# Causal attention: four heads' queries in one tile, scores from 32 rows each, issued for two heads at a time

## The chip, the cores and the metric

The kernel runs on one core of a Trainium2 chip. The time is the device time of one execution in microseconds. The kernel is one program with sixteen stages one after another; the change touches one of them. The engines are called PE (TensorE), DVE (VectorE), ACT (ScalarE), POOL (GpSimd) and SP (SyncE).

## The reference, cut to what matters

The whole computation is a chain of graph and feed-forward layers. The stage at issue is the causal self-attention of the fourth layer: 4 query heads of 32 features over 2 key and value heads, rotary positions, on 16 sequences ("graphs") of 512 tokens with 128 features, all in fp32. The reference text gives its sizes and its rotary tables:

```python
NH, NKV = (4, 2)
HD = C // NH            # C = 128
def _rope_tables(t_len):
    inv_freq = 1.0 / 10000.0 ** (np.arange(0, HD, 2, dtype=np.float32) / HD)
...
def _rotate_half(x):
    h = x.shape[-1] // 2
    return jnp.concatenate([-x[..., h:], x[..., :h]], axis=-1)
```

In words: x is normalised by its mean square, projected to q, k and v; q and k are rotated (q*cos + rotate_half(q)*sin); scores are q k^T / sqrt(32) with only earlier tokens allowed; softmax; times v; output projection; plus x.

## The kernel before, in words

`mha_stage` (L306) with `rope=True` is called once, as stage "mha3". It has one group of four heads. A head has 32 features, so the 128 partitions hold the four heads, 32 each. A graph has 16 items (`items`), one for each of 4 query tiles of 128 tokens and each of 4 heads: item n has head n % 4 and query tile `ORDER[n // 4]`, with ORDER (2, 0, 1, 3). The causal limit makes the items 384, 128, 256 and 512 keys wide, four of each in this order. `all_graphs` runs graph 0, then pairs of graphs in a loop, then graph 15.

Each engine has its own instruction list, and they meet only by semaphores. For item n:

- PE, `scores` (L487): one fp32 matmul from `qT[s][j]` and `kT[s]` into one of two PSUM banks, `score[n % 2]` (an fp32 matmul is two MATMUL records with a weight load each). It waits for `score_taken`, that DVE has taken item n-2 from that bank. Item 0 waits also for `rot_ready`, the rotated k of this graph.
- DVE, `graph` (L800): the "take": score plus mask and the row minimum, into `prob[n % 4]`; after even n a copy of the transposed item n-3 (odd) out of PSUM (L697). A take waits until the transposes of item n-4 are done.
- ACT (L635): the exponential of item n, and after odd n the copy of the transposed item n-3 (even, L606).
- PE, `transposes` (L504): three items behind (`LAG`), one 128x128 transpose for each 128 keys.

`qT[s][j]` is a 128x512 tile for each head j, with the head's 32 rows filled and the other 96 zero. The matmul contracts over all 128 rows against `kT`, which holds all four heads; the zeros take out the other three. The zeros are written once, by eight DVE memsets (L682). With an item n of graph b, PE also issues at fixed places (`at`) a step of the other chains: after item 3 `values` of graph b-1 (L518, 32 matmuls on four column tiles), at 4 `back_rows` (L527), at 6 `turn_ctx` (L533), at 7 `project_out` (L539), at 8 `project_v` (L473), at 9 `rows_in` of graph b+1 (L449), at 10 and 12 two projections each (`early`, L468) of graph b+1. Within one n, `scores(b, s, n)` stands first, then `values`, `transposes(n - 3)`, then the others.

The rotation of graph b+1: PE projects q, q half turned, k, k half turned into the two `misc` banks. DVE multiplies them by the tables (L714, in `rotate`), two at n = 11 and two at n = 13, into `part`. POOL adds the two q products (L409), as four additions of 32 rows, one per head, and then the two k products (L413) into `kT`. At n = 15 DVE has the last step of the statistics, a 128x8 copy (L789), before the take.

## Time and profile before

| | |
|---|---|
| time, median of 3 runs | 5262.46 us (5259.3 to 5265.08) |
| the profiled execution: time / span | 5262.09 us / 5260.3 us |
| PE / DVE / ACT / POOL busy in the span | 75% / 55% / 39% / 32% |
| scores of the stage, L496 (512 records) | 192.6 us busy |
| transposes of the stage, L504 (640 records) | 118.0 us busy |
| takes of the stage, L800 (256) | 125.2 us busy |
| q additions, L409 (64) | 80.9 us busy |
| stage "mha3" in the span | 4088 to 4655 us |

A line of the timeline is one or several instructions of one line of code in a row: start in us from the span's start, length, engine, line, operation, what is written and read, number, and in brackets the idle time of that engine before it and what ended it. Matmul records end with a modelled tail, so the next one can start before the end of one. Windows give the busy time of each engine and the granted clock of PE as a share of 2.4 GHz.

### The profile page before, as it was taken

How to read it: one execution, taken by the hardware profiler on the slowest of the kernel's cores; microseconds unless marked ns; L12 is line 12 of the kernel's file. 1: busy time of each engine (PE TensorE's matmuls, PEld its weight loads, DVE VectorE, ACT ScalarE, POOL GpSimd, SP SyncE). 2: the span in 40 equal slices, each digit the busy share in tenths (PEclk: the TensorE clock that was granted, in tenths of full speed). 3: DMA queues.
4: the chain of work that ended last, by engine and by line, in shares of the span. 5: the costliest groups of instructions: out<-in, count | busy, mean ns of one | idle time of the engine just before them, and what ended most of it. 6: DMA issues, size and time to landing. Idle time of an engine off the chain costs nothing. (4 is left out here: it accounts for less than half of the span.)

```text
span 5260.3 us, 85948 instructions
## 1 busy us (share of the span) xinstructions
PE 3924.9 (75%) x25676; PEld 2535.6 (48%) x25676; DVE 2902.3 (55%) x10746; ACT 2062.9 (39%) x5230; POOL 1658.4 (32%) x1801
## 2 busy tenths in 40 slices
PE   3999978888888539999886776169665677751995
PEld 1333337777777313333364565147554344431663
DVE  5666644444444766666477876322377555543344
ACT  1666643333333005666532266234355344431321
POOL 3445410000000024544362122745522321236444
PEclk9999985555555659999998988589888899965997
DMA  4333349000000023333100021134431000001444
GB/s 131 107 103 111 101 165 382 0 0 0 0 0 0 0 73 104 109 111 98 36 0 1 0 97 41 47 114 145 148 104 41 1 0 0 0 22 51 131 128 157
DMA packets 237304, 376.22 MB, mean 72 GB/s; under 512 B 24832, under 2 KB 157056, under 8 KB 228672
## 3 DMA queue, kind: packets, MB, share of 16 engines
q1 hardware_dynamic: 218688, 336.03, 20.4%
q0 software_dynamic: 18432, 38.05, 2.1%
q8 instruction: 77, 1.26, 0.1%
q14 instruction: 107, 0.88, 0.1%
HBM read 210.37 MB, written 163.61 MB: 71 GB/s over the span
## 5 line engine op out<-in xcount | busy, mean ns | idle before, releaser
L1343 DVE CUSTOM_DVE_ANT_0 mha_seen<-mha_score,mha_mask 128x512 f32<-128x512 f32 x1024 | 686.6, 688 | 454.4 <-PE mha_score L1114 451.5
L1246 ACT ACTIVATE mha_prob<-mha_turned 128x512 f32<-128x512 f32 x1024 | 608.8, 601 | 489.7 <-PE mha_turned L1125 459.3
L1114 PE MATMUL mha_score<-mha_k_rows,mha_q_rows 96*128 96x512 bf16 x1024 | 396.9, 390 | 56.1 <-DVE mha_low L1343 27.8
L3025 POOL DMA_INDIRECT expert_rows<-expert_y,expert_target x320 | 306.4, 957 | 371.6 <-DVE expert_y L3160 155.7
L1124 PE MATMUL mha_turned<-mha_maskT,core_ident_bf 128*128 128x512 bf16 x1024 | 392.8, 384 | 4.6 <-ACT mha_prob L1246 3.5
L1125 PE MATMUL mha_turned<-mha_q_rows,mha_k_rows 99*128 99x512 bf16 x1024 | 390.7, 382 | 0.0
L1498 PE MATMUL lstm_gates<-lstm_h_part,lstm_w_part 128*128 128x16 f16 x4608 | 270.6, 179 | 124.5 <-DVE lstm_h_part L1660 124.4
L1498 PEld LDWEIGHTS lstm_gates<-lstm_h_part,lstm_w_part 128*128 128x128 f16 x4608 | 230.3, 109 | 212.1 <-DVE lstm_h_part L1660 165.1
L1491 PE MATMUL lstm_gates<-lstm_xg,core_ident 128*128 128x48 f32 x1024 | 328.2, 421 | 0.7 <-ACT lstm_xg L1566 0.7
L1448 POOL TENSOR_TENSOR core_mid<-lstm_hist,lstm_per_unit 128x256 f32 x32 | 23.5, 733 | 942.8 <-DVE lstm_hist L1661 942.8
L2698 POOL DMA_INDIRECT routed_rows<-route_rows,core_slot x256 | 253.5, 990 | 151.6 <-issue 78.7
L1652 DVE SCALAR_TENSOR_TENSOR lstm_prod<-lstm_act 128x32 f32<-128x32 f32 x512 | 98.4, 192 | 364.5 <-ACT lstm_act L1572 364.5
L1493 PE MATMUL lstm_out_gates<-lstm_xg,core_ident 128*128 128x16 f32 x1024 | 293.9, 368 | 0.0
L3063 PEld LDWEIGHTS expert_out_ps<-expert_w,expert_hid 128*128 128x128 f32 (+1 forms) x2240 | 262.5, 192 | 38.6 <-issue 36.0
L1493 PEld LDWEIGHTS lstm_out_gates<-lstm_xg,core_ident 128*128 128x128 f32 x1024 | 279.9, 333 | 0.0
L1135 PE MATMUL mha_o<-mha_prob,mha_v 128*32 128x512 f32 x2048 | 272.8, 605 | 1.4 <-ACT mha_prob L1246 1.4
L3063 PE MATMUL expert_out_ps<-expert_w,expert_hid 128*128 128x128 f32 (+1 forms) x2240 | 262.7, 275 | 0.0
L635 ACT ACTIVATE mha_prob<-mha_prob,mha_bias 128x384 f32<-128x384 f32 (+3 forms) x256 | 143.8, 562 | 302.5 <-DVE mha_bias L800 302.1
L800 DVE CUSTOM_DVE_ANT_0 mha_prob<-mha_score,mha_mask 128x384 f32<-128x384 f32 (+3 forms) x256 | 125.2, 489 | 247.2 <-PE mha_tpose L504 126.0
L1491 PEld LDWEIGHTS lstm_gates<-lstm_xg,core_ident 128*128 128x128 f32 x1024 | 257.7, 312 | 1.3 <-issue 1.3
L1572 ACT ACTIVATE lstm_act<-lstm_gates 128x48 f32<-128x48 f32 x512 | 106.5, 208 | 328.4 <-PE lstm_gates L1498 328.4
L1124 PEld LDWEIGHTS mha_turned<-mha_maskT,core_ident_bf 128*128 128x128 bf16 x1024 | 99.5, 97 | 265.5 <-ACT mha_prob L1246 182.6
(477 smaller groups left out, 9130.4 us busy)
## 6 DMA issues: line engine op xcount, KB each, us to landing
routed_rows<-lstm_blank SPq DMA_DIRECT2D x66, 1040.0 KB, 24.9
core_params<-adj SPq DMA_DIRECT2D x32, 1024.0 KB, 5.9
gat_adj_raw<-adj SPq DMA_DIRECT2D x32, 1024.0 KB, 5.5
mha_q_rows<-split_rows SPq DMA_DIRECT2D x64, 384.0 KB, 4.6
mha_k_rows<-split_rows SPq DMA_DIRECT2D x64, 384.0 KB, 5.5
expert_x<-routed_rows SPq DMA_DIRECT2D x80, 260.0 KB
expert_w<-weights SPq DMA_DIRECT2D x80, 256.0 KB
combine_pair<-expert_rows SPq DMA_DIRECT2D x32, 512.0 KB, 4.9
```

Of the source, the lines that this page charges most:

```text
L1114: pe.matmul(score[n % 2][:, :], rows[0][s][0:ROWS, h, t * P:(t + 1) * P], rows[1][s][0:ROWS, h, :], start=True, stop=True).then_inc(S["sco ...
L1124: pe.matmul(turned[n % 2][:, :], core.ident_bf[:, :], maskT[s][:, u, :], start=True, stop=False)
L1125: pe.matmul(turned[n % 2][:, :], rows[1][s][0:ROWS + 3, h, u * P:(u + 1) * P], rows[0][s][0:ROWS + 3, h, :], start=False, stop=True).then_ ...
L1135: last = pe.matmul(o_ps[g][32 * j:32 * j + 32, :], v32[s][:, u, 4 * g + j, :], prob[:, (4 * quad + j) % RING, :], start=(u == 0), stop=(u ...
L1246: act.activation(prob[:, n % RING, :], turned[n % 2][:, :], ACT.Exp, scale=-1.0).then_inc(S["prob_ready"], 1)
L1343: dve.tensor_tensor_reduce(seen[n % 2][:, :], score[n % 2][:, :], mask[1 - s][:, t, :], 1.0, 3e38, ALU.add, ALU.min, low[g][:, t, j:j + 1] ...
L1491: pe.matmul(gates[t % 2][:, 0:3 * B], core.ident[:, :], xg[s][:, t, 1:4, :].rearrange("p g b -> p (g b)"), start=True, stop=False)
L1493: pe.matmul(out_gates[t % 2][:, 0:B], core.ident[:, :], xg[s][:, t, 0, :], start=True, stop=False)
L1498: return pe.matmul(out, w[:, g * P:(g + 1) * P], h_part[:, part, :], start=False, stop=(part == 1 and n in (0, 3)))
L2698: pool.indirect_dma_start(out=rows_dram[:, :], out_offset=bass.IndirectOffsetOnAxis(ap=core.slot[:, i, n:n + 1], axis=0), in_=out_rows[s][ ...
L3025: pool.indirect_dma_start(out=core.y_rows[NUMBER][:, :], out_offset=bass.IndirectOffsetOnAxis(ap=target[q][:, t:t + 1], axis=0), in_=y_buf ...
L3063: last = pe.matmul(out_ps[q % 2][:, t * D:(t + 1) * D], hid[q % 2][0:wid, h, t * P:(t + 1) * P], w_buf[q][0:wid, at2 + h * D:at2 + (h + 1) ...
```

## The change

One tile `qT[s]` holds the queries of all four heads. A score matmul reads the 32 rows of its head from `qT[s]` and from `kT[s]`, so it uses 32 rows of the array, at row 32j. POOL makes `qT[s]` with one addition of 128 rows instead of four of 32. The memsets and their semaphore go. PE issues the scores of items n and n+1 together, at each even n, so that an odd item's matmul, and its wait for `score_taken`, stands ahead of the steps that came between the two. The two items of a pair have different rows and different PSUM banks.

```diff
-        qT = [[m.sb(f"qT{g}{j}", [P, N]) for j in range(4)] for g in range(2)]
+        qT = [m.sb(f"qT{g}", [P, N]) for g in range(2)]
...
                     pool.wait_ge(S["qk_ready"], 4 * b + 2 + 1)
-                    if first:
-                        pool.wait_ge(S["zeros_set"], 8)
-                    for j in range(4):
-                        rows = slice(32 * j, 32 * j + 32)
-                        pool.tensor_tensor(qT[s][j][rows, :], part[rows, 0, :], part[rows, 1, :], ALU.add)\
-                            .then_inc(S["rot_ready"], 1)
-                    pool.wait_ge(S["rot_ready"], 5 * b + 4 + 5)
+                    pool.tensor_tensor(qT[s][:, :], part[:, 0, :], part[:, 1, :], ALU.add).then_inc(S["rot_ready"], 1)
+                    pool.wait_ge(S["rot_ready"], 2 * b + 1 + 2)
                     pool.wait_ge(S["qk_ready"], 4 * b + 4 + 1)
...
                 if n == 0 and rope:
-                    pe.wait_ge(S["rot_ready"], 5 * b + 5 + 5)
+                    pe.wait_ge(S["rot_ready"], 2 * b + 2 + 2)
...
                 pe.wait_ge(S["score_taken"], items * b + n + 1)
                 width = keys(t) * P
                 pair = s if rope else g
-                pe.matmul(score[n % 2][:, 0:width], qT[pair][j][:, t * P:(t + 1) * P], kT[pair][:, 0:width], start=True, stop=True)\
+                head = slice(32 * j, 32 * j + 32)
+                pe.matmul(score[n % 2][:, 0:width], qT[pair][head, t * P:(t + 1) * P], kT[pair][head, 0:width], start=True, stop=True)\
                     .then_inc(S["score_done"], 1)
...
             def graph(b, s, first=False, last=False):
                 for n in range(items):
-                    scores(b, s, n)
+                    if n % 2 == 0:
+                        scores(b, s, n)
+                        scores(b, s, n + 1)
                     if n == at["values"] and not first:
...
-            for q in qT:
-                for j in range(4):
-                    dve.memset(q[j][:, :], 0.0).then_inc(S["zeros_set"], 1)
...
                 if half_ == 0:
-                    dve.wait_ge(S["rot_ready"], 5 * b + 5)
+                    dve.wait_ge(S["rot_ready"], 2 * b + 2)
```

The rest of the diff changes a branch for `rope=False`, which this program doesn't call.

## Rows read from the trace of the kernel before

**Rows 1.** Windows of two neighbouring graphs: busy us (instructions), clock
```profile
4239.70:4273.00 33.30, 24.02 (x141) 14.78 (x141) 18.48 (x60) 13.94 (x42) 7.34 (x7) 1.00 0.00 0
4273.00:4308.00 35.00, 25.60 (x141) 15.76 (x141) 18.67 (x60) 14.02 (x42) 7.34 (x7) 0.95 0.00 0
```

**Rows 2.** PE timeline of the first: start, length, engine, line, operands, idle before
```profile
4239.72 0.91 PE L496 MATMUL mha_score<-mha_kT,mha_qT 128*128 128x384 f32 x2 [1.88 <-POOL mha_kT L413]
4240.46 0.60 PE L504 MATMUL mha_tpose<-core_ident,mha_prob 128*128 128x128 f32 x4
...
4244.43 2.36 PE L518 MATMUL mha_o<-mha_probT,mha_v 128*32 128x512 f32 x32 [0.45 <-DVE mha_probT L697]
...
4254.02 1.16 PE L539 MATMUL mha_misc<-core_params 128*128 128x128 f32 x8 [1.63 <-ACT core_params L628]
...
4258.45 0.63 PE L449 MATMUL mha_misc<-core_ident,core_params 128*128 128x128 f32 x4 [1.29 <-DVE mha_v L721]
...
4261.42 1.99 PE L468 MATMUL mha_misc<-core_params 128*128 128x512 f32 x4 [1.79 <-DVE core_params L705]
...
4265.53 1.98 PE L468 MATMUL mha_misc<-core_params 128*128 128x512 f32 x4 [0.40 <-DVE core_params L714]
4267.35 1.02 PE L496 MATMUL mha_score<-mha_kT,mha_qT 128*128 128x512 f32 x2
4268.22 0.38 PE L504 MATMUL mha_tpose<-core_ident,mha_prob 128*128 128x128 f32 x2
...
4272.98 1.46 PE L496 MATMUL mha_score<-mha_kT,mha_qT 128*128 128x384 f32 x2 [1.87 <-POOL mha_kT L413]
```

**Rows 3.** DVE timeline of the same graph
```profile
4243.59 0.69 DVE L697 COPY mha_probT<-mha_tpose 128x512 f32<-128x512 f32 x1
...
4250.16 0.29 DVE L800 CUSTOM_DVE_ANT_0 mha_prob<-mha_score,mha_mask 128x128 f32<-128x128 f32 x1 [1.67 <-PE mha_score L496]
...
4265.39 0.68 DVE L714 TENSOR_TENSOR core_params<-mha_misc,mha_nsin 128x512 f32<-128x512 f32 x1
...
4268.60 0.69 DVE L800 CUSTOM_DVE_ANT_0 mha_prob<-mha_score,mha_mask 128x512 f32<-128x512 f32 x1 [1.19 <-PE mha_tpose L504]
...
4269.50 1.26 DVE L714 TENSOR_TENSOR core_params<-mha_misc,core_params 128x512 f32<-128x512 f32 x2
...
4271.62 1.26 DVE L789 COPY core_x_stat<-mha_two 128x8 f32 x1
4272.79 0.68 DVE L800 CUSTOM_DVE_ANT_0 mha_prob<-mha_score,mha_mask 128x512 f32<-128x512 f32 x1
```

**Rows 4.** POOL timeline at the end of the same graph
```profile
4266.16 5.27 POOL L409 TENSOR_TENSOR mha_qT<-core_params 32x512 f32<-32x512 f32 x4 [25.57 <-DVE core_params L714]
4271.59 1.26 POOL L413 TENSOR_TENSOR mha_kT<-core_params 128x512 f32<-128x512 f32 x1 [0.16 <-POOL mha_qT L409]
```

**Rows 5.** DVE timeline in the last graph, with POOL idle
```profile
4639.26 0.16 DVE L789 COPY core_x_stat<-mha_two 128x8 f32<-128x8 f32 x1
```

**Rows 6.** Timeline of all engines at the start of the stage
```profile
4091.83 4.27 DVE L682 MEMSET mha_qT<- 128x512 f32 x8 [0.50 <-issue]
...
4096.36 1.09 PE L449 MATMUL mha_misc<-core_ident,core_params 128*128 128x128 f32 x4 [58.19 <-POOL core_params L401]
...
4104.18 0.69 DVE L714 TENSOR_TENSOR core_params<-mha_misc,core_params 128x512 f32<-128x512 f32 x1 [0.16 <-PE mha_misc L468]
...
4109.63 1.01 PE L496 MATMUL mha_score<-mha_kT,mha_qT 128*128 128x384 f32 x1 [5.49 <-POOL mha_kT L413]
```

**Rows 7.** PE timeline in the first attention stage, around column tiles
```profile
331.58 0.38 PE L1125 MATMUL mha_turned<-mha_q_rows,mha_k_rows 99*128 99x512 bf16 x1
331.80 0.38 PE L1114 MATMUL mha_score<-mha_k_rows,mha_q_rows 96*128 96x512 bf16 x1
332.10 1.06 PE L1135 MATMUL mha_o<-mha_prob,mha_v 128*32 128x512 f32 x8
333.10 0.39 PE L1124 MATMUL mha_turned<-mha_maskT,core_ident_bf 128*128 128x512 bf16 x1
```

More of the change, by code:

```diff
@@ L431, in _ @@
             if rope:
-                pool.sem_inc(S["rot_ready"], 5)
+                pool.sem_inc(S["rot_ready"], 2)
             all_graphs(pool, graph)
@@ L598, in _ @@
                 act.wait_ge(S["const_set"], 1)
-                act.wait_ge(S["zeros_set"], 8)
             def copy_probT(b, n):
@@ L615, in take_qk @@
                 else:
-                    for j in range(4):
-                        rows = slice(32 * j, 32 * j + 32)
-                        ins = act.activation(qT[g][j][rows, :], bank[rows, :], ACT.Identity, bias=neg_bq[rows, g:g + 1],
-                                             scale=-scale)
+                    ins = act.activation(qT[g][:, :], bank[:, :], ACT.Identity, bias=neg_bq[:, g:g + 1], scale=-scale)
                 ins.then_inc(S["qk_ready"], 1)
@@ L679, in _ @@
             dve.wait_ge(core.params_in[k], 16)
-            for q in qT:
-                for j in range(4):
-                    dve.memset(q[j][:, :], 0.0).then_inc(S["zeros_set"], 1)
             dve.memset(v32[:, :, :, :], 0.0).then_inc(S["v32_set"], 1)
```

## The prediction, made before the changed kernel was run

> **What bounds the kernel now.** The change touches only the rope attention stage (`mha_stage`, tag mha3), some 550 us of the span from 4090 us on. So I read that stage alone, once the page had shown its slices. First the stretches of two neighbouring graphs [rows 1]: one takes 33.3 us at a granted clock of 1.00, the next 35.0 us at 0.95. PE is the busiest engine (24.0 of 33.3 us), but it is idle for 9.3 us, DVE for 15, POOL for 26. No engine is full; the stage is a chain that passes between them. Of the 15 intervals from one graph's S0 to the next, 6 are of the 35.0 kind, so a fall of the clock costs 1.7 us and comes about in every second graph.
>
> Then PE's timeline of the undisturbed graph [rows 2]. Its waits show where the chain lies: S0 (score matmul of item 0) waits 1.88 us for POOL's kT; the output projection (L539), the turned rows (L449) and the first rotary projections (L468) wait 1.63, 1.29 and 1.79 us for copies by ACT and DVE. I cut the graph at four of these: S0 to values (4239.72 to 4244.43) 4.71 us; values to output projection (4254.02) 9.59; to the turned rows (4258.45) 4.43; to the next S0 (4272.98) 14.53. Sum 33.26.
>
> Last the other two engines at the graph's end. The second rotation on DVE starts at 4269.50 after a wait of 1.19 us for item 13 [rows 3]. POOL's four q additions take 5.27 us from 4266.16, so kT begins only at 4271.59 [rows 4], though the rotation it needs ended at 4270.7. A 128x8 copy on DVE (L789) that starts inside kT's run takes 1.26 us [rows 3]; another, with POOL idle, takes 0.16 [rows 5]. So I read that copy as held until POOL's addition ends.
>
> **Part 1: four q additions become one.** A 32x512 addition takes 5.27/4 = 1.3 us, the 128x512 one for kT 1.26 [rows 4]: cost follows the row length, not the rows. Three of four vanish, 4.0 us of POOL per graph. On the path this is worth less: kT must still wait for the second rotation. Before, kT began 0.9 us after it; after, 0.15 (the step from nsin's end to the first q addition). Gain by this part alone 0.75 us per graph.
>
> **Part 2: no zeros, no memsets.** Eight memsets take 4.27 us of DVE at the stage's start, to 4096.1 [rows 6]. PE's first matmul starts at 4096.36 and waited for POOL's xn, and DVE's next step needs that matmul. POOL's work hides the memsets: gain nothing. The stage's start gains by part 1: the second rotation ends at 4104.8, kT then runs 4104.95 to 4106.2 and S0 starts at 4106.3 instead of 4109.63 [rows 6]: 3.3 us, once.
>
> **Part 3: 32 rows instead of 128.** A score matmul streams the same columns with fewer rows; alone it gains nothing that a row shows. What can gain is that two of them occupy different rows of the array. No row tile is in the trace. The nearest row is the column tiles: eight 512-column fp32 passes on four tiles take 332.10 to 333.10 us, 1.00 us [rows 7], where the two 512-wide fp32 passes of one item on the full array take 0.87, from item 13 at 4267.35 to the transposes at 4268.22 [rows 2]; so four tiles ran nearly together. I take full overlap of the two heads, with none as the other bound. One 512-wide item costs 0.87 us, so 128, 256 and 384 cost 0.22, 0.43, 0.65; a graph's 16 items cost 8.6 us of PE, and paired 4.3.
>
> Against it stands the change of array shape. Into the column tiles the step was 0.30 us [rows 7] where neighbouring full-array steps are 0.22: 0.08 lost. The eight passes, with the way out, took 1.00 us for two passes' 0.87: about 0.1 lost. The tile form appears and leaves eight times per graph, since transposes on the full array stand between pairs. I take 0.1 us for each, bounds 0 and 0.3 (a full exposed weight load and drain). The Trainium skill, TensorEngine Tiling (Array Packing), section Key Properties, says that changing the tiling mode drains the engine. The trace agrees, with 0.08 to 0.1 us.
>
> **Part 4: S(n+1) is issued with S(n).** This moves each odd score ahead of the transposes, projections and values that stood between. Its wait (DVE has taken item n-1) now stands ahead of all of these on PE. I walk the graph with it.
>
> *Rows to next S0.* S10 and S11 follow the turned rows together (+0.1 for the shape). xT's chain on DVE is as before: projections 0 and 1 start at 2.97+0.1 = 3.07 and take 1.99 with tail [rows 2]. Before, item 11 stood behind them and DVE had to take it before the rotation; now it is done. The nsin product begins at 3.07+1.99+0.15 = 5.2 and ends at 5.8 (before 66.0-58.45 = 7.5). S12 and S13 start at 5.2, take 0.87 together, T9 follows, projections 2 and 3 start at 6.6 (before 7.08). DVE takes item 12 at 5.2+1.25 = 6.45 (1.25 is S13 to its take, 4267.35 to 4268.60 [rows 2, 3]). From take 12, which follows nsin at 4266.0, to the rotation (4269.50) DVE had 3.51 us, 1.19 of it the wait for S13, which is gone: 2.32 us. Rotation from 8.77 to 9.95 (before 70.7-58.45 = 12.25). kT 10.1 to 11.35, S0 at 11.5. Before 14.53: gain 3.0.
>
> *S0 to values.* Here the new wait bites: S1 needs item 15 taken. Before, from the rotation's end (4270.7) to take 15 (4272.79) were 2.1 us, with the copy's 1.2. After: take 14 and a copy, 0.95, to 10.9; the 128x8 copy held until 11.4 by kT; take 15 to 12.05. So S1 starts at 12.15, 0.65 behind S0. T13 waits behind it: 12.9 to 13.35 (four transposes, 0.60 with their tail [rows 2]). DVE: copy 13 from 13.6 (0.6), take 1 (0.5) to 14.7. S3 waits for that: 14.8. T15 behind it at 15.55, done 16.2 with its latency, copy 15 (0.6), values at 16.95, which is 5.45 after S0, against 4.71: loss 0.75. (A 512-wide copy is 0.69 in its row and 0.6 from its start to the next one's, a 512-wide take 0.68; the 384-wide take is estimated from it at 0.5 [rows 3].)
>
> *Values to output projection.* S4 enters the shape: +0.1. The take of item 5, 0.29 and its 0.08 [rows 3], stood between the turned outputs and the normalisation, because S5 came behind them; now it lies ahead: -0.4; item 7 no longer starts behind the turned context: about -0.1. 9.15 for 9.59.
>
> *Output projection to rows.* DVE takes items 8 and 9 and v; only the small wait for item 9 goes: 4.2 for 4.43.
>
> **The sum.** 11.5+5.45+9.15+4.2 = 30.3 us for 33.3: 3.0 per graph. Fourteen full intervals give 42; the first gives about the same 3.0 (its first items have no copies before them); the stage's start 3.3; the last graph's loss at its head and gain behind cancel. 48 us. The profiled execution has 5262.09 us (its span 5260.3), 0.4 us from the median of the runs shown, 5262.46. 5262-48 = 5214.
>
> **Rivals.**
> - *The row tiles don't overlap; the change doesn't do what it says.* For: no row shows row tiles. Against: rows 7. Price: S12/S13 +0.87 ahead of the projections, of which DVE's own work covers a part (+0.55), and 0.15 elsewhere: +0.7 per graph, 11 in all: 5225. The forecast hangs little on overlap, since the gain comes from order.
> - *Changing the shape costs 0.3 us, not 0.1.* For: fp32 weights of 128 columns are larger than the 32 columns of rows 7. Six of sixteen changes lie on my walk: +1.2 per graph, 19 in all: 5233.
> - *Evacuation by DVE decides.* Both banks now fill together and empty one after the other; S(n+1) holds the transposes at more places than the head. For: the head shows it at 0.75 us. Against: at six of eight pairs both banks are free by my walk, and DVE is busy 18.5 of 33.3 us. Price, if three more pairs lose as much: +2.25 per graph, 36 in all: 5250. The Trainium skill, TensorEngine Tiling (Array Packing), section PSUM Bottleneck, states such a rule: tiling speeds up the matmuls, and the copy out of PSUM may then be the bound.
> - *The clock falls more often (slower).* PE will be busy about 20 of 30.3 us, 66% for 72% now, and with a lull of 2 us around S0 that is split by single short matmuls. Place: the stage's granted clock, between the two levels 2.4 and 1.2 GHz. A fall costs 1.7 us [rows 1], 6 are there now. It decides from (48+10)/1.7 = 34 falls, over two per graph; at four per graph 16x4x1.7-10 = 99 us: 5313. Against: the longest idle stretches of PE shrink from 1.88 us rather than grow, and the clock stays up between falls now with the same kind of gaps.
>
> **How the numbers follow.** Forecast 0.52 (own range 5196 to 5222), no overlap 0.14, costly shape 0.12, evacuation 0.12, clock 0.10. The low end is the forecast with no falls of the clock left (10 us less) and a change of shape that costs nothing (six on the path, 0.1 us each, 14 graphs, 8 us less): 5196. The high end takes in the costly shape with one fall per graph (9 falls more, 15 us): 5248. What is left out is the clock case and half of the evacuation case, under 2 in 10. About 0.2%, 10.5 us, is what a measurement of this kernel can tell from no change. Below 5251.9: the first three and most of the fourth, 0.84. Within: the rest of evacuation and a mild clock case, 0.08. Slower: 0.08.
>
> **What would show it.** Graph to graph 30.3 us on S0 or kT. POOL: one q addition of 1.26 us, kT within 0.2 us after the second rotation, PE's wait for kT still there, near 1 us. Score passes of two heads starting within 0.05 us of each other, but S1 some 0.6 us behind S0 and S3 behind S2. S0 to values longer, 5.4 us. The second rotation some 10 us after the turned rows. Stage's start to S0 3.3 us shorter. It is wrong if the pair's second matmul regularly waits for DVE, if the clock falls in each graph, or if the rotation still waits for item 13.

## The result, and the profile of the changed kernel

The changed kernel is slower: 5310.28 us (median; 5303.46 to 5317.51) against 5263.77 us of the kernel before on the same chip, a ratio of 1.009 (95% interval 1.0074 to 1.0106), 46.5 us more. The forecast was 48 us less.

First the page of the kernel after: its span, the busy time of the engines and the granted clock in 40 slices. Slices 32 to 35 lie wholly in the changed stage, and the clock is 0.7 in each; in the kernel before these slices have 0.8, 0.9, 0.9 and 0.9.

```profile
span 5315.8 us, 85891 instructions
PE 4000.6 (75%) x25676; PEld 2535.3 (48%) x25676; DVE 2891.7 (54%) x10738; ACT 2065.2 (39%) x5230; POOL 1600.2 (30%) x1753
PEclk8999975555555659999998896599797777765997
```

Next the table of windows. Columns: start and end, length; busy time and count of PE, PEld, DVE, ACT and POOL; granted clock; DMA share and GB/s. The kernel before, from the stage's first S0 to its last score matmul:

```profile
4109.60:4638.70 529.10, 389.66 (x2163) 239.30 (x2164) 285.62 (x919) 219.24 (x662) 109.76 (x90) 0.96 0.00 0
```

The kernel after: the same stretch, then two neighbouring graphs, then the first two rotary projections of the earlier of the two.

```profile
4106.50:4681.60 575.10, 467.05 (x2162) 244.89 (x2162) 277.97 (x918) 221.59 (x664) 52.89 (x45) 0.77 0.00 0
4287.60:4320.60 33.00, 25.54 (x140) 13.78 (x140) 17.75 (x60) 13.95 (x42) 3.45 (x4) 0.90 0.00 0
4320.60:4358.60 38.00, 31.25 (x140) 16.28 (x140) 17.25 (x58) 13.40 (x42) 3.60 (x4) 0.73 0.00 0
4309.70:4313.20 3.50, 3.48 (x4) 1.39 (x5) 1.39 (x5) 0.60 (x2) 0.00 (x0) 0.50 0.00 0
```

The stretch grew by 46.0 us, the size of the medians' difference, and it began 3.1 us earlier. (The two profiled runs, 5317.51 and 5262.09 us, differ by 12 us more than these account for. That lies in the stage behind: from the last score matmul to the last transfer into `routed_rows` it took 229 us for 215, and among all the kernels run here, none of which touches it, 203 to 230.) POOL's work halved, DVE's fell a little, PE's rose from 390 to 467 us with the same count of matmuls. The clock says why: 0.96 before, 0.77 after. With 0.5 for the low level, that is 8% of the stretch at 1.2 GHz before and 46% after. All 14 full intervals from S0 to S0 have the low clock in them: twelve last 36.8 to 38.8 us and two 33.1, mean 37.1. Before, eight of the 14 had none and took 33.3 us [rows 1].

By line, PE's matmuls of the stage, kernel after (line, engine, operation, tiles, count | busy us, mean ns | idle before):

```profile
L500 PE MATMUL mha_tpose<-core_ident,mha_prob 128*128 128x128 f32 x640 | 134.6, 326 | 0.9 <-ACT mha_probT L603 0.9
L463 PE MATMUL mha_misc<-core_params 128*128 128x512 f32 x128 | 99.2, 922 | 24.6 <-DVE core_params L696 24.6
```

and in the kernel before:

```profile
L504 PE MATMUL mha_tpose<-core_ident,mha_prob 128*128 128x128 f32 x640 | 118.0, 285 | 2.2 <-ACT mha_probT L606 2.1
L468 PE MATMUL mha_misc<-core_params 128*128 128x512 f32 x128 | 68.8, 664 | 33.8 <-DVE core_params L705 27.5 <-DVE core_params L714 6.3
```

Neither the transposes nor the projections were edited, yet one takes 326 ns for 285 and the other 922 for 664. Work that the change didn't touch became slower with the clock.

PE's timeline of the graph that starts at 4287.57, kernel after, answers to [rows 2]:

```profile
4287.57 1.46 PE L492 MATMUL mha_score<-mha_kT,mha_qT 32*128 32x384 f32 x4 [0.96 <-POOL mha_kT L408]
4288.96 1.14 PE L500 MATMUL mha_tpose<-core_ident,mha_prob 128*128 128x128 f32 x8
4290.02 1.75 PE L492 MATMUL mha_score<-mha_kT,mha_qT 32*128 32x384 f32 x4
...
4293.24 2.36 PE L514 MATMUL mha_o<-mha_probT,mha_v 128*32 128x512 f32 x32 [0.88 <-DVE mha_probT L688]
...
4302.24 1.16 PE L535 MATMUL mha_misc<-core_params 128*128 128x128 f32 x8 [1.68 <-ACT core_params L622]
...
4306.56 0.63 PE L444 MATMUL mha_misc<-core_ident,core_params 128*128 128x128 f32 x4 [1.27 <-DVE mha_v L712]
...
4309.72 3.78 PE L463 MATMUL mha_misc<-core_params 128*128 128x512 f32 x4 [1.64 <-DVE core_params L696]
...
4320.65 0.58 PE L492 MATMUL mha_score<-mha_kT,mha_qT 32*128 32x384 f32 x1 [0.96 <-POOL mha_kT L408]
```

Cut where the prediction cut, the graph has 5.67 us from S0 to values, 9.00 to the output projection, 4.32 to the turned rows: 18.99, where the walk had 18.8. Then the first two rotary projections (four records) take 3.78 us at a granted clock of 0.50, for 1.99 before [rows 2], and the last part takes 14.09 us instead of 11.5. In most graphs the low clock stays on into the next: there the same values matmuls take 3.85 us, not 2.36. The longest waits there (1.68, 1.27, 1.64 us) are about as long as those of [rows 2] (1.63, 1.29, 1.79), behind which the clock stayed up. Nor was PE less busy. Two windows show the first 20.93 us from S0, first in the undisturbed graph of the kernel before, then in this graph, up to its fall:

```profile
4239.72:4260.65 20.93, 14.70 (x110) 10.29 (x110) 9.99 (x36) 10.23 (x32) 0.86 (x1) 1.00 0.00 0
4287.57:4308.50 20.93, 15.59 (x112) 9.56 (x112) 9.58 (x34) 9.71 (x31) 0.87 (x1) 0.99 0.00 0
```

PE is busy for 70% of the first and 74% of the second, and only behind the second the clock falls. The falls are long, too. One of the kernel before, then the one above and the next:

```profile
4273.30:4276.80 3.50, 3.50 (x11) 2.09 (x10) 1.45 (x6) 1.99 (x5) 0.55 (x1) 0.53 0.00 0
4308.50:4315.30 6.80, 5.58 (x10) 2.12 (x10) 3.28 (x9) 1.57 (x5) 1.00 (x1) 0.53 0.00 0
4321.80:4332.00 10.20, 9.32 (x41) 4.63 (x44) 3.43 (x10) 3.88 (x12) 0.00 (x0) 0.50 0.00 0
```

Read in windows of 0.5 us (not shown), the 14 full intervals hold 26 such falls, 7 to 14 us each and 235 us in all; those of the kernel before hold 6, five of them of 3.4 us and one of 6.8, 24 us in all.

POOL in the same graph, answering to [rows 4]:

```profile
4314.30 1.26 POOL L405 TENSOR_TENSOR mha_qT<-core_params 128x512 f32<-128x512 f32 x1 [25.87 <-DVE core_params L705]
4319.25 1.27 POOL L408 TENSOR_TENSOR mha_kT<-core_params 128x512 f32<-128x512 f32 x1 [3.69 <-DVE core_params L705]
```

One q addition of 1.26 us for four of 5.27, and kT waits for the rotation and not for POOL. So POOL's part of the mechanism worked as told, and the clock took back more than the change gave.

### The profile page after: what moved, and what is told of

It is laid out like the page before. It is cut to its first block and busy times, and to the rows that moved or that the text cites. A ratio compares the mean times of both kernels' runs of the same rounds, so it can differ in the third digit from the quotient of the medians.

```text
span 5315.8 us, 85891 instructions
## 1 busy us (share of the span) xinstructions
PE 4000.6 (75%) x25676; PEld 2535.3 (48%) x25676; DVE 2891.7 (54%) x10738; ACT 2065.2 (39%) x5230; POOL 1600.2 (30%) x1753
## 3 DMA queue, kind: packets, MB, share of 16 engines
q8 instruction: 77, 1.26, 0.1%
```

## The experiments

The question: why does the clock fall in every graph, when PE's longest idle stretches didn't grow? Three theories. *Few rows*: a matmul from 32 rows of the array does not hold the clock as one from 128 does. *Shape*: changing between 32-row and full form, 16 times per graph, leaves holes (packing alone changes it 32 times). *Order*: issuing in pairs makes the lull around S0 worse. The stage column below is the stretch from first S0 to last score matmul in the profiled run, with its clock; the difference is that of the medians on the same chip. The kernel before took 5224 to 5280 us, depending on the chip, so only these differences can be set side by side.

### The change taken apart, and with the array kept at work

**Packing alone, old order** (against the kernel after):

```diff
                 for n in range(items):
-                    if n % 2 == 0:
-                        scores(b, s, n)
-                        scores(b, s, n + 1)
+                    scores(b, s, n)
```

> The changed kernel with the old order: packed queries, one POOL addition, scores from 32 rows, but each score matmul issued alone at its own n. Theory A (the clock falls because 32-row matmuls work a quarter of the array): falls in every graph as in the changed kernel, 35.5 to 37 us per graph, 5290 to 5320 us. Theory B (the clock falls because the pair order makes lulls on PE): clock as before, 0.75 us per graph less for POOL and about as much more for sixteen changes of the array's shape, 5255 to 5270 us. Theory C (not the clock, but changes of shape and the new wait): the sixteen changes alone, about 5270 us.

**Order alone** (against the kernel before: queries with zeros, all 128 rows, four q additions):

```diff
                 for n in range(items):
-                    scores(b, s, n)
+                    if n % 2 == 0:
+                        scores(b, s, n)
+                        scores(b, s, n + 1)
```

> The kernel before with the pair order alone: four zero-padded query tiles, four POOL additions, all 128 rows. Theory A: the clock stays up as before; by my walk the second rotation ends 2.3 us sooner but kT waits for POOL's four additions, S0 comes 1.7 us sooner, the head loses 0.75, the rest gains 0.6: 1.6 us per graph less, about 5238 us. Theory B: falls in every graph, 5290 us or more. Theory C: the new wait costs here too, 5265 to 5300 us.

**The kernel after with fillers**: 28 matmuls per graph whose result nobody reads, on 128 rows and in bf16, put where PE waits (4 ahead of S0, 3 of the values, 4 of the turned outputs, 6 of the output projection, 5 of the turned rows, 6 of the projections).

```diff
+            pe.wait_ge(S["adj_free"], 1)
+
+            def fill(count):
+                for _ in range(count):
+                    pe.matmul(o_ps[1][:, :], core.ident_bf[:, :], mask[0][:, 0, :], start=True, stop=True)
...
+                    if n == 0:
+                        fill(4)
...
                     if n == at["values"] and not first:
+                        fill(3)
                         values(b - 1, groups - 1)
```

> The changed kernel with 28 filler matmuls per graph (bf16, 512 columns, full array, into an unused PSUM bank), placed in PE's waits ahead of S0, values, the turned outputs, the output projection, the turned rows and the first projections. Theories A and B: the granted clock goes back to nearly 1.00 and the graph takes the 30.3 us of my walk, or up to 31.5 where a filler overlaps a wait's end: 5215 to 5240 us. Theory C: no gain, 5310 us or more.

**The kernel before with fillers**: 31 per graph at the same six places (7, 1, 5, 6, 5, 7).

> Control: the kernel before with 31 such fillers per graph in its waits. It has 6 to 9 short falls of the clock in the stage. If fillers hold the clock up they go: 10 us less, about 5253 us; if fillers cost time by themselves it is 5265 us or more.

| kernel | median us | before, same chip | ratio (95%) | difference | stage us, clock |
|---|---|---|---|---|---|
| packing alone | 5476.25 | 5279.73 | 1.038 (1.0363 to 1.0398) | +196.5 | 722.9, 0.67 |
| order alone | 5233.75 | 5279.73 | 0.9917 (0.990 to 0.9933) | -46.0 | 484.1, 0.99 |
| after, filled | 5226.95 | 5279.73 | 0.990 (0.9883 to 0.9916) | -52.8 | 479.0, 0.98 |
| before, filled | 5265.74 | 5279.73 | 0.9976 (0.9966 to 0.9985) | -14.0 | 514.9, 1.00 |

The order is innocent: it saves 46.0 us. Of these, 31 are its 14 graphs at 2.2 us each, and some 8 come from the clock, as two of its graphs have a fall where six had one. The packing does the harm, and far more than I had expected of few rows: 5476.25 us where I had 5290 to 5320. The windows of order alone, one graph and the whole stretch:

```profile
4265.60:4296.60 31.00, 23.79 (x140) 15.04 (x140) 18.72 (x60) 14.04 (x42) 7.26 (x7) 1.00 0.00 0
4117.60:4601.70 484.10, 375.41 (x2161) 237.52 (x2162) 289.98 (x919) 220.00 (x662) 109.77 (x90) 0.99 0.00 0
```

PE is busy for 23.8 of 31.0 us and the clock stays at 1.00. Its POOL still has the old sequence, and kT still comes last on it:

```profile
4289.80 5.29 POOL L409 TENSOR_TENSOR mha_qT<-core_params 32x512 f32<-32x512 f32 x4 [23.35 <-DVE core_params L716]
4295.24 1.26 POOL L413 TENSOR_TENSOR mha_kT<-core_params 128x512 f32<-128x512 f32 x1 [0.16 <-POOL mha_qT L409]
```

With fillers the changed kernel gets its clock back, though they are extra work. The windows of the filled kernel after:

```profile
4292.70:4323.30 30.60, 29.02 (x166) 15.46 (x168) 17.85 (x60) 13.97 (x43) 3.54 (x4) 1.00 0.00 0
4113.40:4592.40 479.00, 454.68 (x2543) 243.26 (x2582) 276.65 (x919) 219.90 (x664) 52.97 (x45) 0.98 0.00 0
```

Its graph at full clock lets the prediction's walk be read off. PE first:

```profile
4292.73 1.46 PE L497 MATMUL mha_score<-mha_kT,mha_qT 32*128 32x384 f32 x4
...
4298.40 2.36 PE L519 MATMUL mha_o<-mha_probT,mha_v 128*32 128x512 f32 x32 [0.23 <-DVE mha_probT L701]
...
4307.40 1.16 PE L540 MATMUL mha_misc<-core_params 128*128 128x128 f32 x8 [0.38 <-ACT core_params L635]
...
4311.72 0.63 PE L449 MATMUL mha_misc<-core_ident,core_params 128*128 128x128 f32 x4 [0.19 <-DVE mha_v L725]
...
4314.88 1.99 PE L468 MATMUL mha_misc<-core_params 128*128 128x512 f32 x4 [0.34 <-DVE core_params L709]
...
4320.38 1.18 PE L497 MATMUL mha_score<-mha_kT,mha_qT 32*128 32x512 f32 x4
...
4323.33 1.14 PE L497 MATMUL mha_score<-mha_kT,mha_qT 32*128 32x384 f32 x3
```

then DVE

```profile
4320.59 1.26 DVE L718 TENSOR_TENSOR core_params<-mha_misc,core_params 128x512 f32<-128x512 f32 x2
...
4322.70 0.52 DVE L793 COPY core_x_stat<-mha_two 128x8 f32 x1
```

and POOL:

```profile
4317.68 1.27 POOL L405 TENSOR_TENSOR mha_qT<-core_params 128x512 f32<-128x512 f32 x1 [24.08 <-DVE core_params L718]
4321.93 1.27 POOL L408 TENSOR_TENSOR mha_kT<-core_params 128x512 f32<-128x512 f32 x1 [2.98 <-DVE core_params L718]
```

The parts are 5.67, 9.00, 4.32 and 11.61 us, 30.6 in all. The fillers fill PE to 29.0 of 30.6 us and stretch the graph by little, since they stand where PE waits. They take 6.6 us of it (six rows of the timeline, not shown); the kernel's own matmuls so have 22.4 of 30.6 us, 73%, as before (72% [rows 1]). Of the 14 us that the same remedy gives the kernel before, some 11 are the six falls that it has in full intervals (the prediction had 10 for them). So the change must be read against before, filled: 5226.95 for 5265.74, 38.8 us. All 14 full intervals are at a clock of 1.00 in both kernels. That is about what the change is worth if the clock doesn't enter.

### Rows or shape

**64 rows instead of 128**, one line of the kernel before. The queries keep their zeros, so nothing else moves.

```diff
                 pair = s if rope else g
-                pe.matmul(score[n % 2][:, 0:width], qT[pair][j][:, t * P:(t + 1) * P], kT[pair][:, 0:width], start=True, stop=True)\
+                two_heads = slice(64 * (j // 2), 64 * (j // 2) + 64)
+                pe.matmul(score[n % 2][:, 0:width], qT[pair][j][two_heads, t * P:(t + 1) * P], kT[pair][two_heads, 0:width], start=True, stop=True)\
```

> The kernel before, old order, zero-padded query tiles and four POOL additions as before; the score matmul alone reads 64 rows (its own head's and a neighbour's, whose queries are zero) instead of 128. Theory A (few rows at work let the clock fall, the more the fewer): between the kernel before and rows_only, 36 to 44 us per graph, 5310 to 5430 us on a chip where before takes 5280. Theory D (changing the array's shape, 32 times per graph, lets it fall): as rows_only, 5450 us or more. If rows don't matter until 32: as before plus the shape changes, 5285 to 5300 us.

**Other shape, same rows**: each score matmul as four column tiles of 32, all 128 rows. It changes the array's form as often as packing alone does.

```diff
-                pe.matmul(score[n % 2][:, 0:width], qT[pair][j][:, t * P:(t + 1) * P], kT[pair][:, 0:width], start=True, stop=True)\
-                    .then_inc(S["score_done"], 1)
+                for c in range(4):
+                    last = pe.matmul(score[n % 2][32 * c:32 * c + 32, 0:width], qT[pair][j][:, t * P + 32 * c:t * P + 32 * c + 32],
+                                     kT[pair][:, 0:width], start=True, stop=True)
+                last.then_inc(S["score_done"], 1)
```

> The kernel before, old order, but each score matmul is cut into four of 32 columns on the four column tiles, all 128 rows. The array's shape changes as often as in rows_only, and the whole array works. Theory A: the clock stays as before; the shape changes cost 0.2 us per item where they are on the path, 1 to 2 us per graph: 5290 to 5315 us where before takes 5280. Theory D: falls as in rows_only, 5450 us or more.

64 rows: 5439.85 for 5260.9 us, ratio 1.0345 (1.0328 to 1.0363), +179 us. Column tiles: 5287.29, ratio 1.0047 (1.0031 to 1.0064), +26.4 us. The whole stretch and one row of PE's timeline of the first:

```profile
4105.40:4806.70 701.30, 611.61 (x2164) 296.02 (x2164) 287.28 (x922) 221.22 (x666) 109.72 (x90) 0.71 0.00 0
```

```profile
4302.11 3.78 PE L468 MATMUL mha_misc<-core_params 128*128 128x512 f32 x4 [1.50 <-DVE core_params L706]
```

and of the second:

```profile
4104.70:4660.70 556.00, 449.85 (x3696) 197.30 (x3700) 286.30 (x919) 219.30 (x664) 110.11 (x90) 0.97 0.00 0
```

```profile
4242.09 0.85 PE L497 MATMUL mha_score<-mha_kT,mha_qT 128*32 128x384 f32 x8
4242.88 0.66 PE L506 MATMUL mha_tpose<-core_ident,mha_prob 128*128 128x128 f32 x4
4243.46 0.85 PE L497 MATMUL mha_score<-mha_kT,mha_qT 128*32 128x384 f32 x8
```

With half the rows the clock falls to 0.71 though order, waits, POOL's and DVE's work are those of the kernel before, and the projections take 3.78 us again. With as many changes of form and all rows it stays at 0.97, and 7 of 14 graphs have a fall for 6; there an item takes 1.37 us (4242.09 to 4243.46) for the 1.18 of the kernel before, which is a cost of the form at full clock. So taking the score matmuls from a part of the rows is the cause, and changes of form as such are not.

Three limits. The 64-row kernel missed its expectation: I had 30 to 150 us over before for few rows, and it was 179, as much as I had given to the theory of shape (170 or more); it is the column tiles that decide between the two. They are not a perfect control, since these longer items keep PE busy for 80% of an undisturbed graph, against 72% before. And the loss doesn't follow the number of rows: 64 rows cost 179 us and 32 rows, one item at a time, 196.5. Whether it is the count of rows or the row-tiled form itself that the clock answers to was not separated.

### The sizes of the other terms

**Filled kernel, first two pairs one by one**: frees the head from the new wait (and 1 filler instead of 3 ahead of the values).

```diff
-                    if n % 2 == 0:
+                    if n < 4:
+                        scores(b, s, n)
+                    elif n % 2 == 0:
                         scores(b, s, n)
                         scores(b, s, n + 1)
```

> The kernel with fillers, with the first four items of each graph issued singly as before and the other twelve in pairs. If the longer way from S0 to values (5.67 us where before has 4.71) is the wait of S1 and S3 for DVE ahead of the transposes, it goes back to 4.7 to 4.9: 0.8 us per graph, 12 us less than the filled kernel, 5215 us. If it comes from elsewhere (DVE's copies, shape changes): no change, 5227 us.

**The same edit on order alone**, where no form changes:

> order_only with the first four items of each graph issued singly. order_only took 5.47 us from S0 to values, before 4.71. If the difference is the wait of S1 and S3 for DVE, 128-row singles bring it back to 4.71 with no shape changes in the way: 0.75 us per graph, 11 us less than order_only, 57 us less than before. If it is not that wait: no change, 46 us less than before.

**Packing alone with the fillers** (old order):

> rows_only with 31 fillers per graph in PE's waits. If the clock is all that made rows_only 197 us slower than before, it comes back to 0.75 us per graph less for POOL and some ten changes of shape on the path at 0.1 us more: 33.5 us per graph, 5270 to 5290 us where before takes 5280. If 32-row matmuls are slow in themselves: 5350 us or more.

| kernel | median us | before, same chip | ratio (95%) | difference | stage us, clock |
|---|---|---|---|---|---|
| filled, head one by one | 5212.26 | 5260.9 | 0.9914 (0.9898 to 0.9931) | -48.6 | 480.5, 0.97 |
| order alone, head one by one | 5173.46 | 5223.64 | 0.990 (0.9883 to 0.9916) | -50.2 | 475.5, 0.98 |
| packing alone, filled | 5318.24 | 5260.9 | 1.0106 (1.0084 to 1.0127) | +57.3 | 589.8, 0.94 |

In the pair kernels S0 to values is 5.47 us (order alone) and goes back to 4.70 with the head one by one: the new wait costs 0.76 us per graph. Its median gained less than that (-50.2 us after -46.0, where I had expected -57); three of its graphs have a fall for two, which explains 2 us of it. In the filled kernel the same edit brought 5.67 down to 5.43 us only, where I had expected 4.7 to 4.9, and the median gained nothing (-48.6 us for -52.8, expected 12 us better); two of its graphs have a fall again. PE's timeline of the filled kernel with the head one by one shows why:

```profile
4279.73 0.90 PE L497 MATMUL mha_score<-mha_kT,mha_qT 32*128 32x384 f32 x2
4280.56 0.66 PE L505 MATMUL mha_tpose<-core_ident,mha_prob 128*128 128x128 f32 x4
4281.15 0.91 PE L497 MATMUL mha_score<-mha_kT,mha_qT 32*128 32x384 f32 x2
...
4285.16 2.36 PE L519 MATMUL mha_o<-mha_probT,mha_v 128*32 128x512 f32 x32
```

An item now takes 1.42 us (4279.73 to 4281.15) instead of 1.18: 0.24 for going into the 32-row form and out of it, 0.12 for each change. Four items one by one hold eight changes where two pairs hold four: 0.48 us more, which eats most of the 0.76 that the wait gave. Packing alone with fillers pays this at all sixteen items: its two graphs without a fall took 35.9 and 36.2 us for 33.3. I had expected 5270 to 5290 us on a chip where before takes 5280, at most 10 us over it, and it was 57 over: besides these 2.6 us, one fall stayed with the fillers in each other graph. Of the +196.5 us of packing alone, then, some 57 remain with the clock mostly restored, and at least the other 139 are the clock's. That packing alone lost more clock than the whole change is likely since an item alone spends twice the time in the 32-row form that it spends beside its neighbour; this was argued and not tried by itself.

### What of a matmul holds the clock

**Fillers from rows 0 to 31 only, and from rows 96 to 127 only**, otherwise the filled kernel:

```diff
-                    pe.matmul(o_ps[1][:, :], core.ident_bf[:, :], mask[0][:, 0, :], start=True, stop=True)
+                    pe.matmul(o_ps[1][:, :], core.ident_bf[0:32, :], mask[0][0:32, 0, :], start=True, stop=True)
```

> The changed kernel with the same 28 fillers in the same places, but from 32 rows instead of 128. PE is as busy in time as in the filled kernel. If what holds the clock up is busy time, it is as the filled kernel, 50 us less than before. If it is the rows at work (theory A), the fillers hold up little: falls in every graph, 35 to 38 us per graph, 10 us less to 60 us more than before.

> The changed kernel with the 28 fillers from rows 96 to 127 instead of 0 to 31 (filled_32: 30 us less than before, with few falls). Theory N: the same as filled_32, 30 us less than before. Theory P: such fillers hold nothing up, as the changed kernel, 45 us more than before.

**One head of four from 32 rows**, in the kernel before: head 0 (items 0, 4, 8, 12), or head 3 (items 3, 7, 11, 15; `slice(96, 128) if j == 3`).

```diff
-                pe.matmul(score[n % 2][:, 0:width], qT[pair][j][:, t * P:(t + 1) * P], kT[pair][:, 0:width], start=True, stop=True)\
+                rows = slice(0, 32) if j == 0 else slice(0, P)
+                pe.matmul(score[n % 2][:, 0:width], qT[pair][j][rows, t * P:(t + 1) * P], kT[pair][rows, 0:width], start=True, stop=True)\
```

> The kernel before, old order; of each four items only that of head 0 reads its 32 rows (0 to 31) alone, the other three all 128. Theory N (the clock goes by how many rows work): a quarter of the loss of rows_only, some 10 to 60 us over before, the same as head3_32. Theory P (it goes by which rows work, and rows 0 to 31 count, since fillers from them held it up): no more falls than before, only 8 shape changes per graph, 5 to 15 us over before.

> The same with head 3 and rows 96 to 127. Theory N: the same time as head0_32 within 10 us. Theory P: falls as if these items were missing, 40 us or more over before, and over head0_32.

**Head 0's items with head 3's rows**, which separates the place in the graph from the place in the array:

> As head0_32, every item of n % 4 == 0 from 32 rows and the others from 128, but these rows are 96 to 127 (head 3's queries and keys in place of head 0's, so head 0's scores are left out and head 3's computed twice; the work has the same size). If the place of the short item in the graph made head0_32 cost 87 us and head3_32 22, it is as head0_32: 80 to 95 us over before. If the rows made it, it is as head3_32: 15 to 30 us over before.

| kernel | median us | before, same chip | ratio (95%) | difference | stage us, clock |
|---|---|---|---|---|---|
| fillers rows 0 to 31 | 5193.39 | 5223.64 | 0.9939 (0.9922 to 0.9955) | -30.3 | 492.6, 0.95 |
| fillers rows 96 to 127 | 5192.39 | 5225.15 | 0.9939 (0.9922 to 0.9955) | -32.8 | 492.7, 0.95 |
| head 0 on rows 0 to 31 | 5312.15 | 5225.15 | 1.0172 (1.0153 to 1.019) | +87.0 | 617.3, 0.79 |
| head 3 on rows 96 to 127 | 5247.39 | 5225.15 | 1.0047 (1.0031 to 1.0064) | +22.2 | 547.9, 0.94 |
| items of head 0, rows 96 to 127 | 5295.45 | 5226.66 | 1.0132 (1.0115 to 1.0149) | +68.8 | 627.3, 0.76 |

(The profiled run of the last kernel took 5327.93 us, so its stage column lies above what its median would have.) Where the 32 rows lie makes no difference to a filler. A quarter of the items on 32 rows cost 87 us at one place of the graph and 22 at another; with the rows exchanged the first place still costs 69. I had expected 10 to 60 us for either head, equal within 10, or 5 to 15 for head 0, and both were wrong. For the exchange I had 80 to 95 if the place decides and 15 to 30 if the rows do: 69 is neither, but nearer to the place, and this kernel's times scatter from 5290 to 5328 us. So the place of the item in the graph weighs most; a smaller share of the rows isn't excluded, and why that place is the sensitive one was not found. 32-row fillers hold the clock at 0.95 over the stretch, with a fall in 4 of 14 graphs, where full ones have 0.98 and none; -30.3 us lies between the two expectations (50 us less than before, or 10 less to 60 more). So added matmuls on few rows help too, if not quite as much; what hurts is few rows in the place of many. What the clock answers to stays open: the fillers are bf16 and the scores fp32, and that was not varied.

### A version that beats both

**kT ahead of the fourth q addition**, on order alone with its head one by one. POOL does q0 to q2, then kT, then q3; S0 waits for kT, and only S3 for q3.

```diff
                         rows = slice(32 * j, 32 * j + 32)
+                        if j == 3:
+                            pool.wait_ge(S["rot_ready"], 5 * b + 3 + 5)
+                            pool.wait_ge(S["qk_ready"], 4 * b + 4 + 1)
+                            pool.tensor_tensor(kT[s][:, :], part[:, 2, :], part[:, 3, :], ALU.add)\
+                                .then_inc(S["rot_ready"], 1)
+                            pool.wait_ge(S["rot_ready"], 5 * b + 4 + 5)
                         pool.tensor_tensor(qT[s][j][rows, :], part[rows, 0, :], part[rows, 1, :], ALU.add)\
                             .then_inc(S["rot_ready"], 1)
...
                 if n == 0 and rope:
+                    pe.wait_ge(S["rot_ready"], 5 * b + 4 + 5)
+                elif n == 3 and rope:
                     pe.wait_ge(S["rot_ready"], 5 * b + 5 + 5)
```

> order_head with POOL's k addition moved ahead of the fourth q addition, and item 3 waiting for that. kT began 1.25 us after the second rotation's end in order_only; now 0.15: 1.1 us per graph, 16 us less than order_head, 73 us less than before in all (ratio 0.986). If the fourth q addition or DVE's taking of item 15 is late then, half of it; if the clock begins to fall each graph, nothing or a loss.

**The same with 25 full fillers** per graph (3, 1, 4, 6, 5, 6):

> k_before_q3 (62 us less than before) with 25 full-array fillers per graph in PE's waits. Its graphs take 29.44 us at full clock and 31.1 where the clock falls, 5 or so of 15. If fillers hold that up: 8 us less than k_before_q3, 70 us less than before (ratio 0.9866). If they reach past the ends of waits: no gain or a loss.

The first has 5161.34 us for 5223.64, ratio 0.9882 (0.9866 to 0.9898), -62.3 us where I had expected -73; the second 5153.5 for 5226.66, ratio 0.9864 (0.9848 to 0.988), -73.2 us where I had expected -70. POOL in the first:

```profile
4282.03 3.93 POOL L415 TENSOR_TENSOR mha_qT<-core_params 32x512 f32<-32x512 f32 x3 [20.84 <-DVE core_params L724]
4286.37 1.27 POOL L412 TENSOR_TENSOR mha_kT<-core_params 128x512 f32<-128x512 f32 x1 [0.41 <-DVE core_params L724]
4287.71 1.27 POOL L415 TENSOR_TENSOR mha_qT<-core_params 32x512 f32<-32x512 f32 x1
```

kT starts 0.16 us behind the second rotation, as in the changed kernel, and the query additions that the packing removes cost nothing any more: POOL has time, only kT's turn mattered. A graph takes 29.44 us, and 31.1 with a fall; the four falls that are left cost 6.5 us, a part of the 11 by which the first missed its expectation. In the second they are gone, as the stretch shows:

```profile
4086.30:4542.40 456.10, 438.47 (x2499) 268.19 (x2538) 275.30 (x919) 221.41 (x662) 111.67 (x91) 1.00 0.00 0
```

Neither packs the queries: the gain comes from order on PE and on POOL, in the second with fillers too, and the matmuls keep their 128 rows.

## Why the prediction was wrong, step by step

**What held.** *Part 1 and the stage's start*: q in one addition of 1.26 us, kT 0.16 behind the rotation (predicted 0.15); S0 of the stage 3.1 us earlier (3.3). *Part 3, overlap*: in the 32-row form two heads' passes run together. In the changed kernel the first two 512-wide passes of a pair take 1.18 us each and 1.19 together at the low clock, and in the filled one a pair's four passes take 1.11 us at full clock (4320.38 to 4321.49), where two items of 0.87 one after the other would take 1.74: full overlap and the two changes of form, 0.87+0.24. The Trainium skill, TensorE: Matmul & The Clock Gate, section Why this matters for your kernels, says that small matmuls on distinct row groups run at the same time; the trace agrees, with 1.19 us for two (its row is below). *Shape*: 0.12 us per change, estimated 0.1. *Part 4*, at full clock, with the filled kernel beside the walk: S0 to values 5.67 for 5.45, values to output projection 9.00 for 9.15, to the turned rows 4.32 for 4.2, to the next S0 11.61 for 11.5; sum 30.6 for 30.3. The second rotation ended 10.04 us after the turned rows (9.95), S1 came 0.55 us behind S0 (0.65), and the wait that this pays for measured 0.76 us per graph (0.75). *The sum* held less well than it seems. The filled kernel is 52.8 us below before, for 48 predicted, but the prediction left before's falls of the clock in place and the fillers remove them. Filled against filled it is 38.8 us, 9 too few: a graph gains 2.7 us (33.3 to 30.6) for 3.0, which is 4 of the 9, and the rest lies at the stage's two ends and was not traced.

```profile
4313.85 1.19 PE L492 MATMUL mha_score<-mha_kT,mha_qT 32*128 32x512 f32 x2
```

**What failed.** The step is the last rival's "Against", and with it its chance of 0.10. "The longest idle stretches of PE shrink from 1.88 us rather than grow, and the clock stays up between falls now with the same kind of gaps." The first half came true (1.68 us at the most in the graph shown) and the clock fell in every graph all the same. The argument looked at when PE is idle, and the change alters what PE does while busy: for the clock, score matmuls on 32 rows did not do what those on 128 did, though PE was busy for as large a share of the time. Run by run: one line that halves the rows costs 179 us, as many changes of form with all rows 26, and the order alone saves 46.

The Trainium skill, TensorE: Matmul & The Clock Gate, section Why this matters for your kernels, gives idle gaps between bursts of matmuls as what to avoid if the clock is to stay up. Here the rule doesn't tell the two kernels apart: their gaps are alike and their clocks 0.96 and 0.77. The measurement decides.

**The rival's price came out right, in part by luck; its reason was wrong.** It had 5313 us for four falls per graph; the median is 5310. Its reason was a lower busy share of PE, "about 20 of 30.3 us, 66% for 72% now". The kernel's own matmuls take 22.4 of 30.6 us at full clock, 73%, no lower than before, and yet the clock fell. Its count was wrong too: not four short falls per graph but about two long ones (26 in 14 graphs), 6.5 us per graph in all (37.1-30.6). Two sizes were off and cancelled. The price was 109 us of falls less the 10 already there, 99, against a gain of 48. Over the stretch the changed kernel's clock costs 575.1-479.0 = 96 us and that of the kernel before 529.1-514.9 = 14, so 82 for 99; and the gain, filled against filled, is 514.9-479.0 = 36 for 48. 82 less 36 is the 46 us by which the stretch grew.

**A choice behind it.** The forecast credited the change with 3.0 us per graph as if its parts belonged together. Order alone at full clock takes 31.06 us per graph, the filled kernel 30.6: packing and the single q addition added 0.5 us per graph to the order's 2.2, and carried all the risk. A sum made for the order alone would have shown how little of the gain hung on the rows.

**The other rivals.** *No overlap* is excluded by the 1.19 us. *Costly shape* (0.3 us) is excluded by 0.12. *Evacuation by DVE* decides at the head alone, as the walk had it; the parts behind the head are as predicted, so no further pair lost to it.

## What to carry to other kernels

Before cutting the rows of a matmul, look at the granted clock of its stage: in a stage whose PE has waits of 1 to 2 us between bursts, matmuls on fewer rows can drop the clock though PE's longest waits don't grow, and every other matmul of the stage pays. Cost the parts of a change by themselves: here the new order, with kT moved ahead on POOL, gave more than the whole change, with less to lose. Where the rows must be cut, matmuls that nobody reads, put where PE waits, can buy the clock back, as they did here with 28 of them per graph.

## What the runs showed of the hardware

- The granted clock went with the rows that the score matmuls use. On the whole stretch: 128 rows 0.96; 64 rows 0.71; 32 rows one item at a time 0.67; 32 rows in pairs 0.77. The scores are fp32 throughout. In the two graphs compared, PE was busier ahead of the fall than where none came (74% and 70% of 20.9 us), and the loss isn't in proportion to the rows.
- The place counts beside the number. A quarter of the items on 32 rows cost 87 or 22 us, by where in the graph they stand.
- Fillers on 32 rows hold the clock almost as well as those on 128 (0.95 and 0.98; 30.3 and 52.8 us below before), wherever their rows lie (492.6 and 492.7 us).
- Going into or out of a 32-row form costs 0.12 us a time between fp32 matmuls of 384 columns (0.24 us for both, halved).
- The 128x8 copy on DVE took 0.52 us in the filled kernel, where it began 0.77 us into kT's addition of 1.27 us, and 1.26 us where it began with it [rows 3]. Both end with the addition: it is held until POOL is through, as the prediction read it.
